# Post-LN transformer layer with routed experts on one core: loop over batches written out, token rows gathered and result rows scattered by GpSimd

## The reference, cut to what matters

```python
def _L0_attn_ref(x, ...):                 # 16 heads of 8, causal
    attn = softmax(where(causal, q @ k.T * head_size ** -0.5, -inf))
    return (attn @ v) @ o_proj_weight.T
def _L0_ffn_ref(x, ...):                  # 64 experts of width 64, top 8 of the 4 best groups
    coef = zeros((T, E)).at[arange(T)[:, None], topk_idx].add(topk_w)
    g = einsum('th,ehi->tei', x, Wg); u = einsum('th,ehi->tei', x, Wu)
    h = silu(g) * u * coef[:, :, None]
    return einsum('tei,eih->th', h, Wd) + silu(x @ SWg) * (x @ SWu) @ SWd
x = layernorm(x + _L0_attn_ref(x))        # x: (8, 512, 128) f32
x = layernorm(x + _L0_ffn_ref(x))
```

## Time and profile before

| | |
|---|---|
| time, median of 2 runs | 1067.7 us (1066.62 to 1068.79) |
| span of the profiled execution | 1066.0 us |
| PE busy | 945.5 us (89%) |
| DVE busy | 810.0 us (76%) |
| POOL busy | 626.2 us (59%) |
| ACT busy | 463.4 us (43%) |

### The profile page before, as it was taken

The page is one execution under the profiler, slowest core; times in us unless marked ns, Lnnn a source line. Parts: engine busy times, 40 slices in busy tenths (PEclk is TensorE's granted clock), DMA queues, the critical chain, the costliest instruction groups (busy, mean ns, idle before and its releaser), DMA issues.

```text
span 1066.0 us, 15603 instructions
## 1 busy us (share of the span) xinstructions
PE 945.5 (89%) x4800; PEld 567.0 (53%) x4800; DVE 810.0 (76%) x2435; ACT 463.4 (43%) x882; POOL 626.2 (59%) x668
## 2 busy tenths in 40 slices
PE   2688689999999979999999879999999979988996
PEld 0233346665565545665566536665566546655653
DVE  4665767799978957789978958789977977588554
ACT  2344335445454434454454435444444435533332
POOL 2432127665676626665676627766577637765775
PEclk7577789999999989999999989999999999999999
DMA  9441144323433224323533225322523222322331
GB/s 295 133 132 53 34 129 147 112 97 107 165 119 102 77 101 165 130 75 112 186 102 113 83 78 179 120 94 77 201 91 117 98 77 83 107 80 76 117 111 58
DMA packets 63069, 120.72 MB, mean 113 GB/s; under 512 B 7056, under 2 KB 34576, under 8 KB 62608
## 3 DMA queue, kind: packets, MB, share of 16 engines
q1 hardware_dynamic: 62992, 119.76, 34.4%
HBM read 97.32 MB, written 22.02 MB: 112 GB/s over the span
## 4 chain that ended last, share of the span: by engine, by line
PE 60%; DVE 28%; issue 5%; DMA 3%; ACT 1%; POOL 1%; SPq 1%; POOLq 0%; DVEq 0%; another core or an unknown queue 0%; PEldq 0%; ACTq 0%
PE acc L663 7%; DVE max_out L959 7%; PE ob L610 7%; PE pg L541 5%; PE pu L541 5%; PE sm L580 5%; PE pg L543 4%; PE pg L542 4%; PE st L598 4%; PE pu L543 4%; PE pu L542 4%; DVE hid L1032 4%; DVE hid L1023 4%; PE acc L653 2%; PE acc L655 2%
## 5 line engine op out<-in xcount | busy, mean ns | idle before, releaser
L775 POOL TENSOR_TENSOR hid<-hid,coef_b 128x512 f32<-128x512 f32 x256 | 332.0, 1297 | 219.9 <-DVE hid L1032 208.9
L724 ACT ACTIVATE hid<-pg 128x512 f32<-128x512 f32 x264 | 157.7, 597 | 376.1 <-PE pg L543 375.5
L959 DVE CUSTOM_DVE_ANT_0 max_out<-sm,causal_sb 128x128 bf16<-128x128 f32 (+3 forms) x512 | 235.8, 483 | 94.7 <-PE sm L580 93.1
L1023 DVE SCALAR_TENSOR_TENSOR hid<-hid,pg 128x512 f32<-128x512 f32 x264 | 180.3, 683 | 112.6 <-ACT hid L724 112.6
L779 POOL TENSOR_TENSOR hid_lo<-hid,hid_hi 128x512 fp32r<-128x512 f32 x128 | 164.1, 1282 | 71.6 <-ACT hid_hi L731 70.2
L696 ACT ACTIVATE probs<-st 128x512 f32<-128x512 f32 (+1 forms) x384 | 187.2, 526 | 24.5 <-PE st L598 22.5
L1032 DVE TENSOR_TENSOR hid<-hid,pu 128x512 f32<-128x512 f32 x256 | 174.8, 683 | 10.2 <-PE pu L543 5.8
L580 PE MATMUL sm<-k_stack,q_stack 72*128 72x128 bf16 (+3 forms) x512 | 140.2, 321 | 34.4 <-DMA k_stack<-k_rows_dram 17.6
L761 POOL TENSOR_SCALAR_AFFINE_SELECT probs<-probs 128x256 f32<-128x256 f32 x256 | 102.2, 423 | 85.5 <-ACT probs L696 84.9
L541 PE MATMUL pg<-x_hi,wg_hi 128*128 128x512 f32 x256 | 139.4, 544 | 8.7 <-DVE hid L1023 8.3
L541 PE MATMUL pu<-x_hi,wu_hi 128*128 128x512 f32 x256 | 124.2, 485 | 16.3 <-DVE hid L1032 16.2
(11 more groups left out here) (129 smaller groups left out, 1216.9 us busy)
## 6 DMA issues: line engine op xcount, KB each, us to landing
coef_b<-coef_dram SPq DMA_DIRECT2D x128, 512.0 KB, 3.9
q_rows_dram<-qk_parts SPq DMA_DIRECT2D x24, 384.0 KB, 3.4
k_rows_dram<-qk_parts SPq DMA_DIRECT2D x24, 384.0 KB, 4.0
q_stack<-q_rows_dram SPq DMA_DIRECT2D x64, 144.0 KB
k_stack<-k_rows_dram SPq DMA_DIRECT2D x64, 144.0 KB
xT_sb<-in_xT SPq DMA_DIRECT2D x8, 256.0 KB, 3.4
y<-in_x SPq DMA_DIRECT2D x8, 256.0 KB, 4.3
out<-out_sb SPq DMA_DIRECT2D x8, 256.0 KB, 2.3
```

What stands on the lines that cost most here:

```text
L775: pool.tensor_tensor(hid[:, i % 3, :], hid[:, i % 3, :], coef_b[:, half % 2, j, :], ALU.mult)\
L959: last = dve.tensor_tensor_reduce(out=max_out[:, seg.nth(BANK_SM, task) % 2, col:col + wide], in0=sm_of(seg, task)[:, col:col + wide], in1 ...
L1023: dve.scalar_tensor_tensor(hid[:, i % 3, :], hid[:, i % 3, :], 1.0, pg[:, :], ALU.add, ALU.mult).then_inc(a_done, 1)
```

## The change

It does two things.

- The three segments become one list, `ALL`, with no hardware loop: the instructions of all eight batches are written out, and the drain, the wait for all DMAs, the clearing of the semaphores and the handshake at the four places are gone. Semaphore counts now run through the whole kernel. `finx` on DVE waits for the store of the batch before it by the same `after` as everything else.
- The load of `y` (SP L436, one DMA of 256 KB per batch) and the store of `out_sb` (SP L491, one of 256 KB per batch) leave SP. GpSimd issues in their place four indirect DMAs each, one per tile of 128 tokens: the row numbers come from a tile `rows_at` [128, 32], written once by an `iota`, and each DMA moves 128 rows of 512 bytes. That is 32 gathers and 32 scatters in GpSimd's in-order stream.

```diff
-    PRO = Segment(prologue_order())
-    BODY = Segment(order(0, 1, range(B)))
-    EPI = Segment(order(6, 7, range(B)))
-    BODY_RUNS = (B - 2) // 2
+    ALL = Segment(prologue_order() + order(0, B - 1, range(B)))
...
+        rows_at = sb("rows_at", [P, B * NT], U32)
...
-        def end_segment(eng):
-            eng.drain().then_inc(seg_done, 1)
-            eng.wait_ge(seg_go, 1)
-            eng.sem_inc(seg_ack, 1)
...
-                    if kind == "ldtok":
-
-                        after(sp, seg, x1_done, ("x1",), seg.last(("x1",), task))
-                        after(sp, seg, out_ready, ("finx",), seg.last(("finx",), task))
-                        sp.dma_start(y[:, :, :], x_tok[base + n]).then_inc(xtok_in, 16)
...
-                sp.wait_ge(seg_done, 4)
-                sp.sem_clear(range(sems[0].num, sems[-1].num + 1))
-                sp.sem_clear(seg_done)
-                sp.sem_inc(seg_go, 1)
-                sp.wait_ge(seg_ack, 4)
...
-            run(pe, tasks)
+            tasks(ALL)
...
+            pool.iota(rows_at[:, :], [[P, B * NT]], base=0, channel_multiplier=1).then_inc(zero_done, 1)
+            pool.wait_ge(zero_done, 3)
...
+                    if kind == "ldtok":
+
+                        after(pool, seg, x1_done, ("x1",), seg.last(("x1",), task))
+                        after(pool, seg, out_ready, ("finx",), seg.last(("finx",), task))
+                        for t in range(NT):
+                            at = bass.IndirectOffsetOnAxis(ap=rows_at[:, n * NT + t:n * NT + t + 1], axis=0)
+                            pool.indirect_dma_start(out=y[:, t, :], out_offset=None, in_=x, in_offset=at)\
+                                .then_inc(xtok_in, 16)
+                    if kind == "finx":
+                        after(pool, seg, out_ready, ("finx",), task)
+                        for t in range(NT):
+                            at = bass.IndirectOffsetOnAxis(ap=rows_at[:, n * NT + t:n * NT + t + 1], axis=0)
+                            pool.indirect_dma_start(out=out, out_offset=at, in_=out_sb[:, t, :], in_offset=None)\
+                                .then_inc(out_stored, 16)
...
-                        dve.wait_ge(last_stored if seg.nth(("finx",), task) == 1 else out_stored, 16)
+                        after(dve, seg, out_stored, ("finx",), ("finx", n - 1, 0), 16 * NT)
```

More of the change, by code:

```diff
@@ L9 @@
 BF16 = mybir.dt.bfloat16
+U32 = mybir.dt.uint32
 ALU = mybir.AluOpType
@@ L453, in tasks @@
                             store_part(kind[0], par, p)
-                    if kind == "rs" and seg is PRO and (n, i) == (0, 0):
+                    if kind == "rs" and (n, i) == (0, 0):
                         sp.wait_ge(zero_done, 2)
@@ L485, in tasks @@
                                      src.unsqueeze(0).to_broadcast([I, 2, 2 * S])).then_inc(c_in[i % 2], 16)
-                    if kind == "finx":
-                        after(sp, seg, out_ready, ("finx",), (kind, n, i))
-                        if seg.nth(("finx",), task) == 1:
-                            sp.sem_clear(last_stored)
-                        sp.dma_start(out_tok[base + n], out_sb[:, :, :])\
-                            .then_inc(last_stored if seg.nth(("finx",), task) == 2 else out_stored, 16)
@@ L494, in finish @@
-            def finish(seg, last=False):
-                if seg is PRO:
-                    sp.wait_ge(w_in, 16 * len(small))
-                for s, kinds, per in ((x_in, ("ld",), 16), (xtok_in, ("ldtok",), 16),
-                                      (parts_stored, ("q", "k"), 16 * PARTS),
-                                      (coef_stored, ("coefT",), 16)):
-                    if seg.total(kinds):
-                        sp.wait_ge(s, seg.total(kinds) * per)
-                for s_all, kind, per in ((stacked, "rs", 16 * 2), (maxrows_in, "mT", 16)):
-                    for j, s in enumerate(s_all):
-                        many = sum(t[0] == kind and t[2] % len(s_all) == j for t in seg.tasks)
-                        if many:
-                            sp.wait_ge(s, many * per)
-                for half in range(2):
-                    many = sum(t[0] == "c" and t[2] % 2 == half for t in seg.tasks)
-                    if many:
-                        sp.wait_ge(c_in[half], 16 * many)
-                if seg.total(("finx",)):
-                    sp.wait_ge(out_stored, 16)
-                else:
-                    sp.sem_inc(last_stored, 16)
-                if last:
-                    sp.wait_ge(last_stored, 16)
-                    return
-                sp.wait_ge(seg_done, 4)
-                sp.sem_clear(range(sems[0].num, sems[-1].num + 1))
-                sp.sem_clear(seg_done)
-                sp.sem_inc(seg_go, 1)
-                sp.wait_ge(seg_ack, 4)
-                sp.sem_clear(seg_go)
-                sp.sem_clear(seg_ack)
@@ L528, in _ @@
-            tasks(PRO, 0)
-            finish(PRO)
-            with sp.Fori(0, BODY_RUNS) as i:
-                tasks(BODY, i * 2)
-                finish(BODY)
-            tasks(EPI, 0)
-            finish(EPI, last=True)
+            tasks(ALL)
+            sp.wait_ge(out_stored, 16 * NT * B)
         @block.tensor
@@ L686, in tasks @@
                         after(act, seg, st_full, ("st",), task)
-                        if seg is PRO and (n, i) == (0, 0):
+                        if (n, i) == (0, 0):
                             act.wait_ge(waiting_free, SPLIT_BY_DVE)
@@ L736, in tasks @@
                         act.activation(ev[:, :], acc[:, :], ACT.Copy).then_inc(acc_free, 1)
-            run(act, tasks)
+            tasks(ALL)
         @block.gpsimd
@@ L780, in tasks @@
                                            ALU.subtract).then_inc(low_done, 1)
-            run(pool, tasks)
+            tasks(ALL)
         @block.vector
@@ L935, in tasks @@
                                 .then_inc(parts_done, 1)
-                    if kind == "v" and seg is PRO and n == 0:
+                    if kind == "v" and n == 0:
                         dve.wait_ge(id_in, 32)
```

47 lines of the change are left out of this document (17 added, 30 removed).

## The result

The changed kernel takes 1115.85 us (1114.44 to 1117.25, two runs) where the kernel before takes 1067.7: a ratio of 1.0476, 95% interval 1.0366 to 1.0585. It is slower by 48 us. The forecast was 1080, with 1104 as the upper end of its range.

A forecast was written before the change was run, and what follows sets the result against it. PE was taken to set the pace. Loop -32.3, gathers +7.7, scatters +32.2 and end +4.2 gave +11.8 us on 1066.0, so 1077.8, given as 1080 for the median of runs; range 1042 to 1104.

The forecast's parts named there:

- p: POOL's time for one indirect DMA, taken as 1.15 us, so a block of four is 4.6 us.
- 60p - 57.2: Change of the whole time in us for a given p, clock term 0.9; slower by over 2% from p = 1.31.
- The stops: PE's waits behind POOL's DMA blocks, per batch: 1.1 us at the gather, 3.7 us at the scatter.
- 4p - 0.9: How late PE's product is behind a block of four scatters: 3.7 us.
- 4p - 3.5: How long PE stands behind a block of four gathers: 1.1 us.
- The sign that it gave: In the changed profile, PE's wait for `hid_lo` behind each scatter would be 2 to 4 us.
- The clock: PE's loss to a lower granted clock: 0.9 us behind each of seven scatter stops, none counted behind gathers.
- The costly rival: At p = 1.46 POOL's blocks stop PE so long that the saving is lost twice: 1104 us, chance 0.31.
- The end: After the last batch, four scatters of 4.6 us replace one store issue of 0.39 us: plus 4.2 us.
- The loop: Writing out the batches removes four segment ends, 5.8, 10.3, 9.2 and 7 us: 32.3 us saved.
- `h` behind the scatter starts about 5 us after `out_sb` is written: Sign expected on POOL in the changed profile: `h` begins about 5 us after `out_sb` is written.
- the change doesn't bring what the loop promises: Rival: written-out streams stop for instructions or batches overlap otherwise, halving the 32.3 us saving: 1096 us, chance 0.04.

The follow-up runs named there:

- a_unroll_sp: The kernel before with its batches written out; SP still loads token rows and stores results by plain DMAs: 1037.93 us, ratio 0.974.
- h_gather_plain: Batches written out, results stored by SP, four plain POOL DMAs per batch in place of the indirect gathers: 1031.47 us, ratio 0.967 to the kernel before.
- dose: Batches written out, loads on SP; two or three of four scatters stay in place, the rest 1.3 units later: 1071.67 us with two, 1083.08 with three.
- j_both_spread: The change with all 64 POOL DMAs kept, each batch's gathers and scatters spread one unit apart: 1050.47 us, ratio 0.986 to the kernel before.
- p_spread_last_on_sp: j_both_spread with the last batch's result stored by SP in one plain DMA: 1047.21 us.
- g_scatter_later: Batches written out, loads on SP, the whole block of four scatters 1.3 units later than in the change: 1063.84 us, ratio 0.998 to the kernel before.
- i_gather_2units_later: b_gather_only with the block of four gathers two units later in POOL's list: 1073.03 us, ratio 1.010 to the kernel before.
- m_scatter_filled: Batches written out, loads on SP, scatters as in the change, ten dead products ahead of PE's wait behind the scatters: 1086.66 us.
- b_gather_only: Batches written out, POOL gathers as in the change, SP stores results by one plain DMA per batch: 1060.96 us, ratio 0.997 to the kernel before.
- e_gather_spread: b_gather_only with each batch's four gathers one unit apart in POOL's list: 1029.45 us, ratio 0.964 to the kernel before.

## Why the prediction was wrong

The forecast of the span was 1077.8 us, and 1115.2 were measured, 37.4 more. By its own steps, with `a_unroll_sp`'s trace as the reference for a kernel without the blocks:

- **p** was taken as 1.15 and is 1.27, inside its bounds (0.42 to 1.46) and on the forecast's side of 1.31. The choice by the nearest rows was good. With the true p the prediction's own 60p - 57.2 gives +19.0, some 1087 us, so p explains 7 us of the miss. The rule it was weighed against, from the Trainium skill, "DMA: Bandwidth & Descriptors", the table of where the 2 us of a software-issued DMA go, has descriptor generation "small, variable". The trace doesn't bear that out for a list of 128 rows: 0.95 us and a gap of 0.30 on POOL, of which the list itself is 0.7 us by `h_gather_plain`.
- **The stops** held. 4p - 0.9 gives 4.2 us for the scatters with the true p and 3.8 to 4.0 were measured; 4p - 3.5 gives 1.6 for the gathers, whose recorded stop is 1.8. For seven batches the prediction had 7 x (1.1 + 3.7) = 33.6 us, and 37.5 came (below). The sign that it gave, a recorded wait of 2 to 4 us, was missed all the same: the idle time is 5.06 us, because PE came to the stop 1.2 us sooner.
- **The clock** is the step that failed. "A 3.7 us stop in which PE first works off other matmuls lies between; I take 0.9", and nothing at all behind the gathers: 6.3 us in all. PE was busy for 969.0 us in the change and for 936.8 in `a_unroll_sp` with the same products, 32.2 us more, 31.1 of them behind the first mark (882.5 against 851.4). Seven periods and the last scatter cost 63.4 + 5.2 = 68.6 us over `a_unroll_sp`, and 68.6 - 31.1 = 37.5 is what the stops took. Counted from the low stretches of a middle period (half of PE's busy time in them), a scatter's stop lost 2.7 us where the prediction had 0.9, and a gather's 1.7 where it had nothing. The fault was to scale the loss with the stop's length, between the two points of the earlier trace rows. The dose shows that it has no such slope: where the clock fell it cost 2.2 us on average, behind 2.5 as behind 5 us, and even the gathers' 1.8 us stop brought 0.57 for 4 us. The costly rival's "full clock loss of 1.7" was too small as well.
- **The end** was put at 4.2 us and took 7.9. The sum had the issues and not what comes behind the last one: 5.5 us from its end to that of the span, where 2.3 us lie behind SP's store in `a_unroll_sp`. With the scatters alone on POOL it is 2.9 us, so most of this comes from having 64 DMAs on POOL and not 32.
- **The loop** was to give back 32.3 us and gave 29.7 in the spans, 26.9 in the medians. By period the four ends were worth 1.7, 8.9, 8.9 and 7.8 us against 5.8, 10.3, 9.2 and 7. The first is the mis-sized one: its period was compared with 116.48 us, but without a segment end it is 120.6 us long by itself.
- 2.4 us lie ahead of the first mark. Nothing can be read from them: the first mark stands anywhere from 127.9 to 134.7 us in the traces here, at 131.7 in `j_both_spread` and 127.9 in `p_spread_last_on_sp`, which are alike up to there.

28.7 (blocks) + 3.7 (end) + 2.6 (loop) + 2.4 = 37.4 us. Of the 28.7, 31.1 - 6.3 = 24.8 are the clock and 3.9 the stops. The range was too narrow for the same reason: it took in both ends of p and only one idea of the clock.

"`h` behind the scatter starts about 5 us after `out_sb` is written" came true, as did "a period without these blocks is 116.5" (but for the first period, and for one of 118.0). The rival "the change doesn't bring what the loop promises" fell with `a_unroll_sp`.

## What to carry to other kernels

Four short jobs in a row on a helper engine are not four times one job. Each alone fits the slack ahead of the bounding engine; together they outlast it, and one unit's distance between them made 64 such DMAs cost 13 us in place of 78. And a stop on PE has two prices, its length and the clock behind it. Price the second from rows with the PE column of equal work, as a lump that may or may not fall due, not as a share of the stop.

## What the runs showed of the hardware

- **The clock behind a stop.** The granted clock was 1.00 behind idle times of 1.51 us (`g_scatter_later`), 2.68 (`i_gather_2units_later`) and 3.00 (`m_scatter_filled`, once), and 0.5 to 0.65 for some 4 us behind 1.84 (`b_gather_only`), 2.54 and 2.87. Another stop of 1.84 us of `b_gather_only` had 1.00 behind it (685.1 to 689.1), and `a_unroll_sp` fell to 0.50 for 3.4 us behind a wait of 1.19 (480.3). The kernel before fell behind its own 3.00 us. So the recorded idle time alone doesn't decide it. The Trainium skill, "TensorE: Matmul & The Clock Gate", section "What's actually happening", says that the clock has two levels, that the low one is the default and that activity releases it. The rows agree as far as they go: the lowest stretch is 0.50, and dead products hold 1.00.
- **Late signals.** Beside the block of gathers ACT and DVE began 2.9 and 2.6 us after the products that they waited for had ended by the trace (the rows at 334.27 and 334.30; "remote" means that the profile has no instruction for what ended the wait), seven times in the change. They were gone with the gathers spread, plain or two units later. What holds them up wasn't found.
- **A DMA where `lo` was.** `e_gather_spread` has periods 0.65 us shorter than `a_unroll_sp`. In the latter a DVE instruction of 16 columns starts together with POOL's `lo` and takes 1.12 us, to the end of `lo`; with a DMA in front of `lo` it takes 0.21. First `a_unroll_sp`, then `e_gather_spread`:

```profile
432.51 1.28 POOL L714 TENSOR_TENSOR hid_lo<-hid,hid_hi 128x512 fp32r<-128x512 f32 x1
...
432.70 1.12 DVE L918 TENSOR_TENSOR max_parts<-max_rest,max_parts 128x16 bf16<-128x16 f32 x1
```

```profile
433.08 0.21 DVE L923 TENSOR_TENSOR max_parts<-max_rest,max_parts 128x16 bf16<-128x16 f32 x1
433.09 1.05 POOL L693 DMA_INDIRECT y<-in_x,rows_at  x1 [0.16 <-issue]
```

  The Trainium skill, "SBUF — State Buffer", section "SBUF: two separate sides", has a DVE instruction with two inputs in SBUF and a GpSimd instruction that reads SBUF take turns on a shared pair of ports, each for its whole length. The trace agrees: 433.79 is the end of `lo` and 433.82 that of the DVE instruction. In `h_gather_plain`, whose periods are 115.8 us as well, the DVE instruction takes 0.17 us there. That these 0.9 us make the 0.65 us of the period was not tested by itself.
